# The tail of an attention megakernel: last head's transposes in the score banks, subtractions moved ahead, a value sum in three pieces

## What is computed

```python
# 1. cross attention, 16 heads of 64; the residual is added
q, k, v = x_norm @ w_q, ctx @ w_k, ctx @ w_v            # per head
x1 = x + softmax(q k^T / 8) v @ w_o
# 2. retention, 8 heads of 16, with a decay mask, group norm and a gate
Q, K = xpos(xn1 @ W_Q), xpos_inverse(xn1 @ W_K);  V = xn1 @ W_V
Y  = ((Q K^T) * decay) V                                # "head products" below
x2 = x1 + (silu(xn1 @ W_G) * groupnorm(Y)) @ W_O
# 3. four binary trees of depth 8 (q, k, v, f) choose one of 256 leaves per row
leaf(t, z): walk the tree, h = act(z @ w1[leaf] + b1), return h @ w2[leaf] + b2
q, k, v = leaf(q, xf), leaf(k, xf), leaf(v, xf)         # xf: x2 normalised, 16 blocks each
y   = xf + softmax(q k^T / sqrt(128)) v
out = x2 + y + leaf(f, y)
```

## Time and profile before

| | |
|---|---|
| median of three runs | 648.92 us (647.2 to 649.37) |
| the profiled execution | 648.99 us, of which the span on the core is 647.1 us |
| PE busy | 615.1 us (95% of the span) |
| DVE busy | 470.8 us (73%) |
| ACT busy | 393.4 us (61%) |
| POOL busy | 263.6 us (41%) |
| chain that ended last, by engine | PE 66%, POOL 13%, DVE 9%, ACT 5%, DMA 3%, issue 3% |

### The profile page before, as it was taken

One profiled execution on the slowest core, in us unless ns is written; L12 is line 12 of the kernel. 1 busy time (PEld: TensorE's weight loads), 2 busy tenths in 40 slices (PEclk: granted clock), 3 DMA queues, 4 the chain that ended last, 5 costly groups with the idle time before them and its releaser, 6 DMA issues.

```text
span 647.1 us, 10067 instructions
## 1 busy us (share of the span) xinstructions
PE 615.1 (95%) x3752; PEld 511.9 (79%) x3755; DVE 470.8 (73%) x846; ACT 393.4 (61%) x834; POOL 263.6 (41%) x252
## 2 busy tenths in 40 slices
PE   8899999999999999998999999998999999888887
PEld 5678888888888888877888888877888878785674
DVE  3656667778778677878676878878777877866863
ACT  3756655676765555786655865767554955741571
POOL 2210000230302102997526154997343257974633
PEclk9989999999999999999999999999999999999999
DMA  8910000011200003540030017240030008011933
GB/s 192 247 34 1 1 1 1 0 35 33 66 1 1 1 1 125 212 134 1 1 136 2 0 32 265 109 134 2 1 135 2 2 4 324 12 70 49 352 142 139
DMA packets 21399, 48.49 MB, mean 75 GB/s; under 512 B 1508, under 2 KB 14696, under 8 KB 17256
## 3 DMA queue, kind: packets, MB, share of 16 engines
q0 software_dynamic: 4608, 34.74, 14.5%
q1 hardware_dynamic: 16456, 12.99, 7.7%
q10 hardware_dynamic: 288, 0.13, 0.1%
HBM read 47.59 MB, written 0.26 MB: 74 GB/s over the span
## 4 chain that ended last, share of the span: by engine, by line
PE 66%; POOL 13%; DVE 9%; ACT 5%; DMA 3%; issue 3%; POOLq 0%; DVEq 0%; ACTq 0%
PE ps_s L472 23%; PE ps_av L472 20%; PE ps_ring L747 14%; PE ps_m L472 4%; PE ps_ring L472 4%; POOL leaf L1591 4%; DVE chunk_max L1438 2%; POOL leaf L1595 2%; ACT prob L1096 2%; DMA w_room<-down_v_dram,idx 2%; DVE pt L1181 2%; POOL ct_lo L1560 2%; ACT pt L1026 1%; DMA leaf<-down_f_dram,idx 1%; DVE hid L1250 1%
## 5 line engine op out<-in xcount | busy, mean ns | idle before, releaser
L1026 ACT CAST pt<-ps_ring 128x512 fp32r<-128x512 f32 x256 | 144.6, 591 | 153.5 <-PE ps_ring L747 153.3
L1181 DVE TENSOR_TENSOR pt<-ps_ring,pt 128x512 fp32r<-128x512 f32 x256 | 170.4, 686 | 48.3 <-ACT pt L1026 48.1
L472 PE MATMUL ps_av<-pt,c_hi 128*128 128x512 f32 (+1 forms) x544 | 188.6, 393 | 1.2 <-issue 1.2
L1096 ACT ACTIVATE prob<-ps_s,neg_max 128x1024 f32<-128x1024 f32 x128 | 141.7, 1115 | 23.0 <-DVE neg_max L1525 22.9
L747 PE MATMUL ps_ring<-ident,prob 128*128 128x128 f32 x1024 | 144.9, 274 | 10.6 <-DVE x_sb L1470 4.3
L1438 DVE TENSOR_REDUCE chunk_max<-ps_s 128x1 f32<-128x1024 f32 x128 | 150.7, 1216 | 3.9 <-PE ps_s L472 3.8
L747 PEld LDWEIGHTS ps_ring<-ident,prob 128*128 128x128 f32 x1024 | 117.4, 141 | 37.2 <-issue 24.3
L472 PE MATMUL ps_av<-pt,c_lo 128*128 128x256 f32 x512 | 143.1, 279 | 0.0
L472 PEld LDWEIGHTS ps_av<-pt,c_hi 128*128 128x128 f32 x544 | 100.0, 188 | 21.2 <-issue 2.3
L472 PE MATMUL ps_s<-ct_hi,q_hi 128*128 128x512 f32 x256 | 113.2, 442 | 2.9 <-ACT prob L1096 1.6
L472 PE MATMUL ps_s<-ct_hi,q_lo 128*128 128x512 f32 x256 | 102.1, 399 | 0.0
(11 more groups left out here) (293 smaller groups left out, 720.8 us busy)
## 6 DMA issues: line engine op xcount, KB each, us to landing
stage<-ctx_t_dram SPq DMA_DIRECT2D x16, 256.0 KB, 4.0
stage<-ctx_rows_dram SPq DMA_DIRECT2D x16, 256.0 KB, 3.1
leaf<-w_v_dram SPq DMA_DIRECT2D x1, 512.0 KB, 9.0
leaf<-w_o_dram SPq DMA_DIRECT2D x1, 512.0 KB, 10.9
dec<-decay_dram SPq DMA_DIRECT2D x1, 512.0 KB
nw<-node_w_dram SPq DMA_DIRECT2D x1, 510.0 KB
wsm<-w_small_dram SPq DMA_DIRECT2D x1, 448.0 KB
leaf<-wq_t_dram SPq DMA_DIRECT2D x1, 320.0 KB, 10.8
```

Of the source, the lines that this page charges most:

```text
L472: return nc.tensor.matmul(o, l, r, start=start, stop=stop)
L1026: nc.scalar.copy(pt_hi[:, pp, row:row + KPC, P * (n % 2):P * (n % 2 + 1)], ps_ring[:, i % 2, :].rearrange("p (k q) -> p k q", k=KPC)).then ...
L1096: nc.scalar.activation(prob[:, n % 2, 1024 * e:1024 * (e + 1)], ps_s[:, 1024 * e:1024 * (e + 1)], ACT.Exp, bias=neg_max[:, n:n + 1], accum ...
L1181: return nc.vector.tensor_tensor(o, a, b_, op)
```

## The change

Five things are edited.

- **Transposes.** The four groups of the last head, 63, are transposed into the four banks of `ps_s`, which no scores need any more (`last_transposes`), and no longer into the ring. ScalarE and VectorE read them there (`upper_last`, `lower_last`). The drain's order on TensorE becomes: all transposes first, then the four quarters of pair 31.
- **ScalarE and VectorE in the drain.** Both follow `LAST_CASTS`: ScalarE casts the first group of head 62 ahead of the exponential of head 63, and its eight leaf products come behind all casts. VectorE does the seven remaining subtractions first, and then the softmax sums, the hidden layer, "out0" and the output of pair 30.
- **The last loop slot on VectorE.** The first half of head 63's maximum comes ahead of a hidden layer, and the two subtractions of head 61 ahead of the second half.
- **"out1"** moves out of the drain to number 74, between the statistics of `x1` and the normalisation of the fourth entry.
- **The value sum** is cut in three: the bias and blocks 8 to 12 ("v_first", 75.5), blocks 13, 14, 15 and 0 ("v_more", 79), blocks 1 to 7 ("v_rest", 79.5); "attv" goes from 79 to 80. The first half of the fourth entry's head products goes to `ps_ring` in place of `ps_av`.

```diff
 BEFORE_LAST_AT = {
-    ("PE", "qk_t"): 72, ("PE", "att"): 73.5, ("PE", "v_half"): 73, ("PE", "v_rest"): 76, ("PE", "attp_t"): 76, ("PE", "attv"): 79, ("PE", "y_t"): 80,
+    ("PE", "qk_t"): 72, ("PE", "att"): 73.5, ("PE", "v_first"): 75.5, ("PE", "v_more"): 79, ("PE", "v_rest"): 79.5, ("PE", "attp_t"): 76, ("PE", "attv"): 80, ("PE", "y_t"): 80,
...
-    ("DVE", "out1"): 1000,
+    ("DVE", "out1"): 74,
...
+LAST_CASTS = ((HEADS - 2, 1), (HEADS - 2, 2), (HEADS - 1, 0), (HEADS - 1, 1), (HEADS - 2, 3), (HEADS - 1, 2), (HEADS - 1, 3))
...
+VALUE_BLOCKS = {"v_first": (8, 9, 10, 11, 12), "v_more": (13, 14, 15, 0), "v_rest": (1, 2, 3, 4, 5, 6, 7)}
...
-            return ps_s[:, 512:512 + P // 2] if second else ps_av[:, 0:P // 2]
+            return ps_s[:, 512:512 + P // 2] if second else ps_ring[:, 0, 0:P // 2]
...
+            def last_transposes(g):
+
+                pe.wait_ge(S["exp_done"], 2 * (HEADS - 1) + g // 2 + 1)
+                for i in range(KPC):
+                    k = (KPC * g + i) * P
+                    last = nc.tensor.transpose(ps_s[:, k:k + P], prob[:, (HEADS - 1) % 2, k:k + P], ident[:])
+                last.then_inc(S["last_turned"], 1)
...
                 transposes(HEADS - 2, 0)
-                transposes(HEADS - 2, 1)
                 pe.wait_ge(S["ring_free"], BY_DVE[("T", HEADS - 3, 3)])
                 context_quarter(before, 2)
-                transposes(HEADS - 1, 0)
+                transposes(HEADS - 2, 1)
                 context_quarter(before, 3).then_inc(S["av_done"], 1)
-                transposes(HEADS - 1, 1)
                 transposes(HEADS - 2, 2)
+                last_transposes(0)
+                last_transposes(1)
+                transposes(HEADS - 2, 3)
+                last_transposes(2)
+                last_transposes(3)
                 pe.wait_ge(S["av_taken"], PAIRS - 1)
...
+                for quarter in range(CH):
+                    pe.wait_ge(S["ring_free"], BY_DVE[("T", HEADS - 2, quarter)])
+                    pe.wait_ge(S["last_free"], quarter + 1)
+                    done_quarter = context_quarter(last, quarter)
...
+                if s == HEADS:
+                    upper_pt(HEADS - 2, 0)
                 if 0 <= n < HEADS:
...
+                    for head, g in LAST_CASTS:
+                        if (head, g) == (HEADS - 1, 0):
                             take_context(PAIRS - 2)
...
+                        if head == HEADS - 1:
+                            upper_last(g)
+                        else:
+                            upper_pt(head, g)
+                    down_part(B - 2, 1, 0, 8)
...
+                    lower(HEADS - 2, 0)
+                    for head, g in LAST_CASTS:
+                        if head == HEADS - 1:
+                            lower_last(g)
+                        else:
+                            lower(head, g)
+                    weights(PAIRS - 2)
+                    weights(PAIRS - 1)
+                    hidden_layer(B - 2, 2)
+                    leaf_output(B - 2, 0)
+                    add_output(PAIRS - 2, HEADS + 1)
...
+                if n == HEADS - 1:
+                    max_half(n, 0)
                 for k, b in steps_at(DVE_AT, s, 0):
                     rest(k, b)
+                if n == HEADS - 1:
+                    lower(tr, 2)
+                    lower(tr, 3)
```

More of the change, by code:

```diff
@@ L547, in value_sum @@
                     pe.wait_ge(S["v_weighed"], 1)
-                    for l in range(LW // 2, LW):
-                        mm(o, ident[:], rows[:, D * l:D * (l + 1)], False, False)
-                else:
+                elif piece == "v_more":
                     pe.wait_ge(S["weighed"], 4 * (B - 2) + 3)
-                    for l in range(LW // 2):
-                        last = mm(o, ident[:], rows[:, D * l:D * (l + 1)], False, l == LW // 2 - 1)
+                blocks = VALUE_BLOCKS[piece]
+                for l in blocks:
+                    last = mm(o, ident[:], rows[:, D * l:D * (l + 1)], False, piece == "v_rest" and l == blocks[-1])
+                if piece == "v_rest":
                     last.then_inc(S["v_summed"], 1)
@@ L688, in rest @@
                     third_sum()
-                elif k in ("v_half", "v_rest"):
-                    value_sum(k == "v_half")
+                elif k in VALUE_BLOCKS:
+                    value_sum(k)
                 elif k == "qk_t" and b < B - 1:
@@ L1027, in upper_pt, with upper_last @@
                                ps_ring[:, i % 2, :].rearrange("p (k q) -> p k q", k=KPC)).then_inc(S["hi_done"], 1)
+            def upper_last(g):
+                act.wait_ge(S["last_turned"], g + 1)
+                pp, row = part(PAIRS - 1, KPC * g)
+                nc.scalar.copy(pt_hi[:, pp, row:row + KPC, P:2 * P],
+                               ps_s[:, 512 * g:512 * (g + 1)].rearrange("p (k q) -> p k q", k=KPC)).then_inc(S["hi_done"], 1)
             def take_context(pair):
@@ L1433, in lower, with lower_last @@
                    ALU.subtract).then_inc(S["ring_free"], 1)
+            def lower_last(g):
+                his[0] += 1
+                dve.wait_ge(S["hi_done"], his[0])
+                pp, row = part(PAIRS - 1, KPC * g)
+                at = (slice(None), pp, slice(row, row + KPC), slice(P, 2 * P))
+                tt(pt_lo[at], ps_s[:, 512 * g:512 * (g + 1)].rearrange("p (k q) -> p k q", k=KPC), pt_hi[at].bitcast(F32),
+                   ALU.subtract).then_inc(S["last_free"], 1)
             def max_half(n, e):
@@ L1526, in _ @@
                                             negate=True).then_inc(S["negmax_ready"], 1)
-                if trs:
+                if trs and n < HEADS - 1:
                     lower(tr, 2)
```

54 lines of the change are left out of this document (11 added, 43 removed).

## The result

| | median | runs | against before, 95% interval |
|---|---|---|---|
| before | 648.81 us | 22 | |
| changed kernel | 650.01 us (648.65 to 652.26) | 22 | 1.0034 (1.0023 to 1.0046) |
| changed kernel, again, beside the last experiments | 650.15 us | 12 | 1.0033 (1.0016 to 1.0050) |

The change makes the kernel slower by 0.34%, 2.2 us of 648.8; the plain medians lie 1.2 us apart, the means 2.1.

The account below looks back on a forecast made before the run. TensorE was taken to hold two thirds of the chain, with pauses in the drain, then a chain of single steps. 648.99 - 2.5 (the drain's 3.75 included) + 4.0 + 1.7 = 652.2 us; range 649.3 to 654.2.

Parts of the forecast that it names:

- the signs to look for: New profile: context near 575.2, fourth entry's transpose near 580.3, ScalarE idle over 2 us, y near 592 or later, clock about 0.5.
- The drain, -3.75: After the loop, TensorE's pauses mostly go and ScalarE takes the last context at 575.2 instead of 578.95: 3.75 us less.
- the two waits left in the sum: In the drain: head 62's second group waits for a ring half; pair 31's first quarter for head 63's first cast and subtraction.
- To the transposed rows, -2.5: From the context to the fourth entry's transpose, "out1" costs 0.2 and holds "qk_t"; transpose at 580.3 against 582.84, 2.5 us less.
- The value sum, +4.0: Between scores and sums of squares, the three pieces and their later copy make the first sum 4.0 us later, bounds 3.5 and 4.5.
- steps (d) and (e): ScalarE's squares wait behind the value sum's copy (592.95), VectorE's sums of squares behind y (593.75): first sum 4.0 us later.
- Without the clock, +1.5: Drain to transposed rows and value sum together, -2.5 + 4.0 = +1.5, or 650.5 us, if TensorE keeps its speed.
- The clock, +1.7: From 575.1 to 581.0 TensorE, without the value sum's first half, is little busy; clock falls, 1.7 us more, bounds 0 and 2.6.
- Behind the gated rows: After the gated rows' transpose at 593.50 nothing is edited; the shift up to there is added unchanged to 648.99 us.
- The clock that stays up (650.5): Rival 1: TensorE's clock does not fall in the emptier stretch, so 650.5 us; chance 24%.
- the late sum holds nobody: Rival 2, ScalarE and VectorE before the roots: squares start with the head products, 1.9 us less, 647.1; chance 7%.
- the drain fails: Rival 3: casts and subtractions become the bound and push GpSimd's work; 1 to 2 us on top, 653.7; chance 9%.

Follow-up runs that it names:

- the last experiments: Runs beside the changed kernel's second timing, among them twelve warm-up matmuls added to it (1.0008) and the new drain with old value sum and more warm-up matmuls (0.9953).
- the drain run alone: Changed kernel with the value sum put back as it was before, without warm-up matmuls: 0.9998 of before.
- the kernel with the filler: Changed kernel plus twelve warm-up matmuls that compute nothing, ahead of the third entry's two transposes ("qk_t"): 1.0028 of before, run again 1.0008.
- the squares: Changed kernel with ScalarE's squares ahead of the value sum's copy and the fourth entry's chain ahead of y: 1.0003 of before; with twelve warm-up matmuls 0.9991.
- the sum ahead of the products with more fillers: Changed kernel with warm-up matmuls, early "xn1_t" and the value sum complete before the head products, plus six later warm-up matmuls: 0.9961 of before (0.9965 without the six).
- the two orders that kept both chains early: New drain with warm-up matmuls: old value sum (0.9969, with more warm-ups 0.9953), or value sum complete ahead of the head products (0.9965, with more 0.9961).

## Why the prediction came out as it did

The sign, the range and the signs to look for were right; the forecast, 3.2 us above the profile of before, was 1 us more than the timed 2.2 (and 652.2 lies 2.2 above the median, 650.01).

- **The drain, -3.75.** Right in mechanism, -4.30 measured. Mis-sized: the two waits left in the sum, 1.0 us together, were some 0.5, by start-to-start distances (0.08 ahead of head 62's second group, 0.41 ahead of pair 31's first quarter).
- **To the transposed rows, -2.5.** Measured -2.81 and -2.43. "out1" costs the normalisation nothing (0.2 forecast), and it holds "qk_t" as forecast. The size holds for the whole change; as the drain's own gain, which I expected of the drain run alone (-2.5 to -2.8), it failed: with the old value sum it is -0.14, and with fillers -1.69 where the changed kernel with fillers has -2.92. The rest belongs to the value sum, which no longer stands ahead of "xn1_t".
- **The value sum, +4.0.** With the clock up, the way from "xn1_t" to the gated rows is 14.81 us against 10.66, +4.15. Taking the squares and y apart gives 3.5 of it back, with the clock up in both (36.49 to 33.01); the 5.30 and 4.08 us of idle time ahead of the copy and y are the forecast's steps (d) and (e). The Trainium skill (TensorE: Matmul & The Clock Gate, "Architectural detail") calls ScalarE and VectorE strict queues; these two rows agree.
- **Without the clock, +1.5.** Measured +1.23 at the gated rows in the kernel with the filler.
- **The clock, +1.7.** Measured 1.31 with a fall of 3.4 us and 2.46 with one of 6.8, 1.4 in the timed runs side by side. The size holds, the reason only in half. Taken alone, the new value sum does empty the wait that its blocks had filled, and the clock falls, as forecast. But with the old value sum in the new drain it falls as well: the blocks that I had called a filler stand behind "qk_t" and are weighted only at the stretch's end. The idle time of the changed kernel comes from the drain ending earlier while "out1" now stands ahead of "qk_t" behind the last output, and leaving the blocks where they were would not have covered it.
- **Behind the gated rows** I took the shift as constant. It grew from 2.54 to 3.41 us in the profile. The kernel with the filler, whose clock stays up, has 0.85 of such growth too; its gather of the q rows is issued 1.23 us later than before and GpSimd starts on the k rows 1.86 later (54.14 from W against 52.28), waiting for their transfer. So part of it is transfers, which the sum left out.
- **Rivals.** The clock that stays up (650.5) is nearest to the median, but by luck: its mechanism is refuted by the clock rows. That the late sum holds nobody is refuted by the squares. That the drain fails is refuted by the context at 574.65.

What stays open is why the clock fell in the profile of the sum ahead of the products with more fillers, and how much of the 1 us between forecast and timed result is the transfers and how much the clock, which is not the same in every execution (mean of a run 0.987 to 0.997). Before varies too: 14 of its 28 timed runs beside the first experiments have a mean clock of 0.995, below the 0.997 of its profile, and none of those was kept as a trace. So the profiles' 3.41 may be larger than the timed 2.2 because the profile of before has no fall behind W. Not run apart are the edits of the drain itself (the score banks, the order of casts and subtractions, the moved maximum), and no run puts "out1" in another place.

## What to carry to other kernels

A part of a change can gain only because another part moved work out of its way: run each half alone before its gain is added up, and look what stands first in the queue of the engine that was freed. When an engine is freed earlier but its next input isn't, ask whether the work put there as cover is ready by then; here matmuls without inputs did cover, and the value blocks did not. And where two chains share the transfers, speeding one up by delaying the other gained nothing here: the two orders that kept both chains early, with fillers, were the fastest (0.9953 to 0.9969, not to be told apart). Before two profiles are subtracted, look whether the clock was low for equally long in both.
